# The instruction order of TensorE set anew in a Mamba and SwiGLU kernel on one core

## The reference, cut to what matters

```python
def mamba(x):                       # x: 8 batches x 512 tokens x 128 features, f32
    h = x * rsqrt(mean(x*x) + 1e-5) * norm_w
    xs, res = split(h @ in_proj_w.T)            # 256 channels each
    u = silu(causal_conv4(xs) + conv_b)
    delta, Bm, Cm = split(u @ x_proj_w.T, [64, 16, 16])
    delta = softplus(delta @ dt_proj_w.T + dt_proj_b)
    state = exp(delta*A)*state + (delta*u)*Bm   # scan over the tokens, 256 channels x 16 states
    y = sum_over_states(state * Cm) + u*D
    return (y * silu(res)) @ out_proj_w.T + x
x = layernorm(x + mamba(x))
x = layernorm(x + (silu(x @ wg.T) * (x @ wu.T)) @ wd.T)   # 384 hidden, int weights / 127
```

## Time and profile before

| | us |
|---|---|
| median of three runs (lowest, highest) | 560.69 (560.64, 561.02) |
| the profiled execution | 562.91 |
| its span, first to last instruction | 561.1 |
| PE busy in the span | 522.8 (93%) |
| DVE busy | 495.8 (88%) |
| POOL busy | 414.2 (74%) |
| ACT busy | 385.8 (69%) |
| mean granted TensorE clock | 0.963 |

### The profile page before, as it was taken

How to read it: one execution, slowest core, us unless ns; L and a number is a source line. 1 busy time by engine, 2 the same in 40 slices (tenths; PEclk the granted TensorE clock), 3 DMA queues, 4 the chain that set the end, 5 groups by cost and what they waited for, 6 DMA issues and landing times.

```text
span 561.1 us, 7049 instructions
## 1 busy us (share of the span) xinstructions
PE 522.8 (93%) x2161; PEld 272.9 (49%) x2161; DVE 495.8 (88%) x559; ACT 385.8 (69%) x625; POOL 414.2 (74%) x212
## 2 busy tenths in 40 slices
PE   8989998999999999999999999999999997668695
PEld 6444444545564536545564536544564534433363
DVE  5867789998999999999999999999999999998863
ACT  3676896599478975699478974799478974554231
POOL 8769677996579874996589874996589874996310
PEclk9979999999999999999999999999999999759798
DMA  8062305600624032700624032600634042700000
GB/s 224 9 151 56 96 8 143 151 0 2 150 59 111 1 73 78 167 4 0 151 62 108 0 82 70 169 0 0 150 63 106 0 90 60 168 2 0 0 20 19
DMA packets 27391, 39.29 MB, mean 70 GB/s; under 512 B 3832, under 2 KB 10072, under 8 KB 27360
## 3 DMA queue, kind: packets, MB, share of 16 engines
q1 hardware_dynamic: 25168, 38.38, 28.7%
q10 hardware_dynamic: 2192, 0.55, 0.5%
HBM read 3.27 MB, written 2.10 MB: 10 GB/s over the span
## 4 chain that ended last, share of the span: by engine, by line
PE 74%; DVE 9%; issue 6%; ACT 5%; POOL 2%; DMA 1%; SPq 1%; POOLq 0%; DVEq 0%; ACTq 0%
PE dense_ps L508 18%; PE y_ps L500 9%; PE dense_ps L526 9%; PE dense_ps L577 7%; DVE state L1196 6%; PE dense_ps L584 3%; PE c_ps L484 3%; PE dense_ps L528 2%; PE dense_ps L533 2%; PE dense_ps L545 2%; PE y_ps L498 2%; PE dense_ps L547 2%; PE dense_ps L551 2%; PE dense_ps L549 2%; PE dense_ps L541 2%
## 5 line engine op out<-in xcount | busy, mean ns | idle before, releaser
L1018 POOL TENSOR_TENSOR prod<-du_rep,b_rep 128x2048 f32<-128x2048 f32 x63 | 286.0, 4544 | 71.9 <-ACT b_rep L778 50.0
L1196 DVE TENSOR_TENSOR_SCAN state<-decay_ps,prod 128x512 f32<-128x512 f32 x256 | 298.9, 1207 | 17.3 <-ACT decay_ps L731 10.6
L731 ACT ACTIVATE decay_ps<-delta_rep,a_neg 128x512 f32<-128x512 f32 x252 | 170.0, 689 | 71.8 <-DVE state L1196 71.6
L1206 DVE TENSOR_TENSOR state<-state,c_ps 128x1536 f32<-128x1536 f32 (+1 forms) x63 | 122.8, 1949 | 19.0 <-PE c_ps L484 14.8
L508 PE MATMUL dense_ps<-x_all,ident 128*128 128x256 f32 x476 | 121.8, 398 | 5.6 <-ACT z_pos L757 3.6
L508 PEld LDWEIGHTS dense_ps<-x_all,ident 128*128 128x128 f32 x476 | 88.5, 195 | 48.4 <-issue 15.6
L500 PE MATMUL y_ps<-state,gather 128*32 128x512 f32 x504 | 70.8, 635 | 4.6 <-DVE state L1206 4.6
L526 PE MATMUL dense_ps<-h_t,tap_t 128*128 128x512 f32 x128 | 58.4, 598 | 0.9 <-ACT h_t L789 0.9
L1040 POOL TENSOR_TENSOR state<-state,c_rep 128x512 f32<-128x512 f32 x40 | 51.4, 1285 | 4.3 <-ACT c_rep L774 4.2
L484 PE MATMUL c_ps<-bc,pick 64*128 64x512 f32 x64 | 31.6, 493 | 8.4 <-DVE state L1206 8.4
L526 PEld LDWEIGHTS dense_ps<-h_t,tap_t 128*128 128x128 f32 x128 | 23.2, 189 | 30.5 <-issue 29.4
(11 more groups left out here) (201 smaller groups left out, 691.3 us busy)
## 6 DMA issues: line engine op xcount, KB each, us to landing
du_rep<-z_wm SPq DMA_DIRECT2D x64, 256.0 KB, 5.0
delta_rep<-z_ln SPq DMA_DIRECT2D x64, 256.0 KB, 4.5
out_dram<-y_out SPq DMA_DIRECT2D x7, 256.0 KB, 4.7
state<-L_attn_in_proj_w_in ACTq DMA_DIRECT2D x1, 256.0 KB, 3.9
x_all<-L_attn_x_in SPq DMA_DIRECT2D x1, 256.0 KB, 4.2
state<-L_ffn_w_gate_in SPq DMA_DIRECT2D x1, 192.0 KB, 10.0
state<-L_ffn_w_up_in SPq DMA_DIRECT2D x1, 192.0 KB, 3.5
state<-L_ffn_w_down_in SPq DMA_DIRECT2D x1, 192.0 KB, 4.3
```

Source lines behind the costliest of these rows:

```text
L731: A(decay_ps[n % DECAYS][:, :], decay_ps[n % DECAYS][:, :] if spread_first else delta_rep[:, h, c, :], ACT.Exp, scale=a_neg[:, col:col + 1 ...
L1018: TT(prod[quad % 2][:, :, :], du_rep[:, h, :, :], b, ALU.mult).then_inc(prod_ready, 1)
L1196: dve.tensor_tensor_scan(state[n // BLOCKS % 2][:, n % BLOCKS, :], decay_ps[n % DECAYS][:, :], prod[n // BLOCKS % 2][:, n % BLOCKS, :], 0. ...
L1206: TT(state[quad % 2][:, mine, :], state[quad % 2][:, mine, :], c_ps[:, :].unsqueeze(1).broadcast_to([P, BLOCKS - mine.start, T]), ALU.mult ...
```

## The change

TensorE's order, its banks, the steps of the other engines, and the list of shared quads are replaced. A steady batch had 32 idle products and has 30. SHARED goes from quads 1, 2, 4, 5, 6 to quads 0, 1, 4, 5, 6 (five either way, and the same three copies of C). In the head, b3 goes from bank 0 to bank 2. In the tail the idle products before the transposes go from 6 to 5. No operation of the computation is added or removed.

```diff
-        PLAN = [["Fh", "Fh", "Fh", "Fh", "Fh", "Fh", "Fh", "Fh", "C", "Fh", "S", "h"],
-                ["proj", "xs0", "C", "S", "xs1"],
-                ["res0", "res1", "C", "Fxd", "Fxd", "Fxd", "Fxd", "Fxd", "S"],
-                ["xd", "Fz0", "Fz0", "S", "x1", "Fz0", "Fz0", "z0", "C"],
-                ["z1", "Fgate0", "Fgate0", "Fgate0", "Fgate0", "Fgate0", "S", "Fgate0", "Fgate1", "Fgate1", "Fgate0", "Fgate0", "Fgate1", "gate0", "C", "gate1", "d0"],
-                ["S", "gate2", "C", "d1", "b0"],
-                ["up0", "up1", "up2", "S", "Fb1", "b1", "C", "down", "Fb2", "Fb2"],
-                ["b2", "b3", "C", "S"]]
-        BANK = {"h": 1, "xs0": 1, "proj": 2, "xs1": 0, "res0": 2, "res1": 1, "xd": 2, "z0": 1, "z1": 2, "x1": 0,
-                "gate0": 1, "up0": 2, "gate1": 2, "up1": 0, "gate2": 1, "up2": 2, "b0": 1, "b1": 0, "down": 2,
-                "b2": 0, "b3": 1, "d0": 0, "d1": 0}
-        ACT_AT = {"hx": 1, "y": 4, "h": 3, "r1": 7, "silu": 9, "xd": 13, "x1n": 11, "z": (16, 17), "x1": 16,
-                  "ze": 17, "zw": 19, "zwm": 20, "ln": 21, "gate": (20, 22, 23), "b": (25, 28, 31, 31), "down": 29,
-                  "d": (23, 25), "c": 2}
-        DVE_AT = {"combine": (18, 1), "stats1": 7, "gate": (20, 22, 23), "up": (25, 26, 26), "stats2": 29}
-        POOL_AT = {1: [], 2: ["C1"], 3: ["norm1", "C2"], 4: ["low"], 5: ["C4"], 6: ["scale0", "C5"], 7: ["C6"],
-                   8: ["scale1", "norm2"]}
+        PLAN = [["Fh", "Fh", "Fh", "Fh", "Fh", "Fh", "Fh", "Fh", "h", "C", "S"],
+                ["Fxs0", "Fxs0", "xs0", "proj", "C", "S", "xs1", "res0", "res1"],
+                ["S", "C", "Fxd"],
+                ["Fz1", "xd", "Fz0", "Fz1", "Fz0", "z0", "C", "x1", "S", "Fz1"],
+                ["z1", "Fgate0", "Fgate0", "Fgate0", "Fgate0", "Fgate0", "Fgate1", "Fgate0", "Fgate0", "C", "S", "gate0"],
+                ["gate1", "d0", "C", "S", "Fup0", "gate2", "d1", "Fb0"],
+                ["up0", "b0", "up1", "Fup2", "up2", "C", "S", "Fb1", "b1"],
+                ["down", "Fb2", "Fb3", "b2", "b3", "C", "S"]]
+        BANK = {"h": 0, "xs0": 1, "proj": 0, "xs1": 0, "res0": 2, "res1": 1, "xd": 1, "z0": 2, "z1": 0, "x1": 1,
+                "gate0": 1, "up0": 2, "gate1": 2, "up1": 0, "gate2": 1, "up2": 2, "b0": 1, "b1": 1, "down": 0,
+                "b2": 2, "b3": 1, "d0": 0, "d1": 0}
+        ACT_AT = {"hx": 0, "y": 2, "h": 1, "r1": 5, "silu": 9, "xd": 12, "x1n": 12, "z": (13, 15), "x1": 14,
+                  "ze": 16, "zw": 16, "zwm": 18, "ln": 19, "gate": (19, 19, 21), "b": (24, 28, 31, 31), "down": 28,
+                  "d": (20, 24), "c": 2}
+        DVE_AT = {"combine": (19, 2), "stats1": 7, "gate": (20, 20, 22), "up": (24, 26, 26), "stats2": 29}
+        POOL_AT = {1: ["C0"], 2: ["C1"], 3: ["norm1"], 4: [], 5: ["low", "C4"], 6: ["scale0", "C5"],
+                   7: ["C6", "scale1"], 8: ["norm2"]}
-        STIR_TAIL = {"S": 7, "x1": 6, "gate0": 0}
+        STIR_TAIL = {"S": 7, "x1": 5, "gate0": 1}
-        SHARED = [1, 2, 4, 5, 6]
+        SHARED = [0, 1, 4, 5, 6]
-        HEAD_BANK = {... "b1": 0, "b2": 2, "b3": 0}}
+        HEAD_BANK = {... "b1": 0, "b2": 2, "b3": 2}}
```

More of the change, by code:

```diff
@@ L291, in mamba_swiglu_postln @@
         HEAD_JOBS = ["h", "xs0", "res0", "xs1", "res1", "xd", "z0", "z1", "b0", "du0", "du1", "b1", "b2", "b3"]
-        HEAD_BANK = {**BANK, **{"h": 2, "xs0": 1, "res0": 2, "xs1": 0, "res1": 1, "xd": 2, "z0": 0, "z1": 1, "b0": 2, "du0": 0, "du1": 2, "b1": 0, "b2": 2, "b3": 0}}
+        HEAD_BANK = {**BANK, **{"h": 2, "xs0": 1, "res0": 2, "xs1": 0, "res1": 1, "xd": 2, "z0": 0, "z1": 1, "b0": 2, "du0": 0, "du1": 2, "b1": 0, "b2": 2, "b3": 2}}
         FFN_JOBS = ["gate0", "gate1", "gate2"]
```

## The result

The changed kernel takes 558.84 us (median of 20 runs, 554.52 to 561.72), the kernel before 560.76 (20 runs, 558.89 to 562.78): a ratio of 0.9963, 95% interval 0.9949 to 0.9977. It is faster, by 1.9 us; 7.7 were forecast. The profiled execution took 558.52 us with a span of 556.8, against 562.91 and 561.1 before, 4.4 us less; the one before lay 2.2 above its median, so the two profiles flatter the change.

What follows compares the result with a forecast made beforehand. TensorE, busy 62.50 of 63.00 us, was taken to bound the steady batch. Six batches at -1.0, batch 0 -1.7 and batch 7 -0.5 make -8.2, less the later first scan -7.7: 553.0 us, range 549 to 559.5.

Steps and rivals of the forecast that it cites:

- (a): Steady batch, TensorE: two idle products fewer, 32 to 30, save 0.86 us; bounds 0 and -1.26.
- (d): Steady batch: a new TensorE wait at x1 costs 0.5 us and a later C 0.1; bounds 0 and +1.6.
- (b): Steady batch, TensorE: fewer changes of product kind, but new steps between C and S; together 0, bounds -0.4 and +0.4.
- (c): Steady batch: TensorE's waits for reads of z, xs0 and bank 2 go, -0.82 us; bounds 0 and -0.85.
- So the loop stays on TensorE, with half a microsecond to spare: Steady batch: VectorE, exponential 1 and hx have h ready at 65.0, 0.5 us before TensorE's h at 65.4.
- Batch 0 ... -1.7; TensorE waits some 1.6 us for hx there: End of batch 0: first scan of batch 1 moves from 99.04 to 97.35, -1.7 us; bounds 0 and -2.5.
- Batch 7, "-0.5": Last batch, without in jobs: some VectorE waits shrink, new ones of 1.2 and 1.4 come; net -0.5, bounds +2 and -2.5.
- The runs' median lies 2.2 below it: Whole kernel: the runs' median lies 2.2 us below the profiled execution, turning 555.2 into 553.0.
- the 0.5 that the sum had taken off for the later first scan: Sum of terms: a first scan 0.6 us later in its batch takes from the gain once, -8.2 to -7.7.
- Rival 1: TensorE's clock falls once in each steady batch, at the wait for x1 or h: 573 us, chance 0.09.
- rival 2: A new wait (VectorE's loop to h, or x1n) holds the period near 62.8: 558.5 us, chance 0.20.
- The rule of the Trainium skill: Against the forecast: fewer idle products and waits at h and x1 could halve the clock in each batch.

Runs made afterwards that it cites:

- e5: The kernel before with two idle products fewer a batch, 30 instead of 32 (one Fxd, one Fgate0): 556.93 us, ratio 0.9941.
- e11: As e10, with 26 idle products a steady batch instead of 30: 551.29 us, ratio 0.984 to the kernel before.
- e1: The changed kernel run again, unchanged: 557.14 us, ratio 0.9954 to the kernel before.
- e4: The changed kernel with ScalarE reading b1 at step 27 instead of 28: 556.92 us, ratio 0.9939 to the kernel before.
- e2: The changed kernel with batches 3 to 6 written out instead of looped: 555.81 us, ratio 0.9933 to the kernel before.
- e3: The changed kernel, loop kept, with h placed behind C and S in quad 0: 557.39 us, ratio 0.9939 to the kernel before.
- e9: As e2, plus six idle products on b2's bank in batch 0, where other batches have down: 556.01 us, ratio 0.9925 to the kernel before.
- e7: The changed kernel written out and with b1 read at step 27: 557.89 us, ratio 0.9939 to the kernel before.
- e10: As e9, plus eight idle products ahead of up2 in batch 7: 554.88 us, ratio 0.9897 to the kernel before.
- e8: As e7, plus idle products in batch 7 where those of the missing in jobs had fallen away: 557.38 us, ratio 0.9936 to the kernel before.

## Why the prediction was wrong, step by step

- **The steady batch, (a) to (d): right in sum.** The period of an undisturbed steady batch came out at 62.0 for 61.9. The two products alone gave 0.7 of the 0.86 (e5), and the rest of the change 0.2, as (b) to (d) add up to. The wait for z_pos went; x1 waits 0.27, forecast 0.5. VectorE's new waits are at scan 11 (0.30, forecast 1.0), gate0 (0.41) and gate2 (0.48). The small terms of (b) and (c) were not measured one by one.
- **"So the loop stays on TensorE, with half a microsecond to spare": right where no turn of the loop is, and the step that failed.** h started 3.56 us into the batch as worked out. With four products less the period fell by 0.6 instead of 1.7, and TensorE waited (e11), so the spare half microsecond is real. But the step took ScalarE to bring hx on time in every batch. In batch 5 it does not: the 1.25 us stop at the loop's turn is longer than the slack, TensorE waits 1.80, and the clock falls. All three profiles with the loop and h in front have it (the result, e1, e4), none of the written-out ones has. The old kernel's ScalarE came late there too: the first of three exponentials ahead of hx starts 2.6 us before the first scan (350.61), where the same one starts 4.4 before it in batch 3 (220.44 against 224.84), a wait that the profile puts down to VectorE. But h stood behind C, an idle product and S and did not wait, and its batch 5 took 63.1:

```profile
348.02 1.91 ACT L731 ACTIVATE decay_ps<-delta_rep,a_neg 128x512 f32<-128x512 f32 x3 [2.07 <-DVE state L1196]
```

```profile
351.92 0.66 PE L519 MATMUL dense_ps<-ident,hx 128*128 128x128 f32 x4
```

Price in the profiles: 3.7 us (e1 against e2), of which about three by the order of h (e3); in the medians it is not told apart. The old trace named no stop, but its batch 5 was 0.2 longer than the others. I took the mean of six batches and did not ask what a piece of work moved to the first step of the loop body would meet.
- **"Batch 0 ... -1.7; TensorE waits some 1.6 us for hx there": mis-sized, the second step that failed.** -0.6 in the profile, and batch 1 takes 63.93, 1.9 more than the steady ones. With the head's clock low for 6.8 us in both profiles the first scan went from 99.04 to 98.47. In e1 it stood at 97.26, as forecast, but by luck: its head had no low clock, and batch 1 still took 64.20. I took the first scan as what counts, though TensorE bounds the batches: even at full clock it waits for hx (1.41 in e4, 1.09 in e9), and batch 1 takes 62.55, some 0.5 more than the others. The fall of the clock adds 1.1 to 1.6 (63.7 to 64.2 where it is low for 6.8 us; in e2 it is low for 3.4 us, the wait for hx covers that, and batch 1 takes 62.55). It came not with the wait for hx but with 1.6 us of standing before it, at the read of b1 and at C, which the forecast hadn't. It does not come in each execution (e4 and e7), and in none of three where the gap is filled (e9, e10, e11).
- **Batch 7, "-0.5": off the other way in the profile, open in size.** -3.8 in the two profiles, but the batch took from 57.2 to 61.8 us in the profiles of this order, so the -3.8 is a lucky draw in part. Every profile has the gap ahead of up2 and a fall of the clock at its end, unless it is filled (e10, e11); the longest forms are those in which it stays low until down's products, 3.4 to 4.0 us of them instead of 2.84 (e3, e7, e8). The wait of 1.4 forecast at gate2 is there in four profiles of nine.
- **"The runs' median lies 2.2 below it": a step without ground.** It took the distance between one profile and the median of three runs as a constant. After the change the profiled execution lay 0.3 below its median. Of the 5.8 us between 553.0 and 558.84 this step makes 2.5. The other 3.3 are in the profiles (558.5 for 555.2): against the forecast 61.94 a batch, 3.8 in batch 5, 2.0 in batch 1 and 0.2 in the other four, and 1.1 at the first scan, less 3.3 that batch 7 did better and less the 0.5 that the sum had taken off for the later first scan.
- **Rival 1 gave the mechanism, rival 2 the time.** The clock does fall behind TensorE's waits, but at two batch borders, not in each batch; 558.5 was rival 2's figure (its own sum, 560.7 - 2.5, gives 558.2), for another reason than the one I gave: the period was not held near 62.8. Its "about 1.5 us" of waits stood between the 0.50 without a fall and the 1.66 with one before. The 1.80 of batch 5 (a fall in three profiles of three) and the 1.64 of batch 0 fit it; the 1.85 of e11, the 2.15 in the head of e1, and the 0.31, 1.42 and 1.41 within ten microseconds of e4, all without a fall, show that it is no bound.
- **The rule of the Trainium skill.** The Trainium skill, page "TensorE: Matmul & The Clock Gate", section "A second HAM failure mode: psum-queue depth-cycling", says that short idle times between groups of products, if frequent, can make the clock swing between its two levels. Waits of 0.4 to 0.5 us, two in each batch, left it at 1.00 for 369 us (e11), so the traces do not bear it out at that size and rate. The falls at the end of batch 0 and in batch 5 came behind single waits of 1.4 to 1.8 us, and not behind each of that length.

What stays open: why the same waits end in a fall in one execution and not in another, and how the difference between profile (4.4 us) and median (1.9 us) divides. The fastest runs of the changed kernel had a mean clock of 0.973 and took 554.5, the slowest 0.955 and 561.7. Batch 7 took from 57.2 to 61.8 us in the profiles of the new order at 30 products and from 59.0 to 61.0 in those of the old, but the share of each place in the median was not measured.

## What to carry to other kernels

A work item moved to the very start of a loop body can lose its slack against the loop's own turn; look at the one iteration behind the turn, not at the average one. Idle products that are there to keep the clock up cost up to their full time where TensorE is the bound (two of them 0.7 us in e5, where they add up to 0.86): find how few hold it, before reordering. Price each new wait of TensorE twice, as a wait and as the work that may then run at half the clock. And before one profile's stretch is called a gain, look at where the clock was low in it: two profiles of one kernel (the result, e1) differed by 1.2 us at the first scan of batch 1, behind a head with and without a low clock.

## What the runs showed of the hardware

- ScalarE stood still for 1.25 and 1.07 us with no semaphore to wait for, between the second and third instruction of the hx behind the turn of the loop; in the written-out kernel the stop is gone (e2), and hx runs through in 1.26 us.
- The same instructions with the same waits kept the clock at 2.4 GHz in one execution and lost it in another: 0.31 and 1.42 us in e4 against 0.30 and 1.42 in e7, and 2.15 us in e1 against 2.14 in the profile of the result, which are one kernel. Its 20 runs lay from 554.52 to 561.72 us, the fastest with a mean clock of 0.973, the slowest with 0.955.
- A stretch at 1.2 GHz need not cost time: in e2 the clock is low from 89.7 to 93.1 us, and batch 1 lasts 62.55 as in the executions without a fall there, since a wait of TensorE stood behind it.
